# Sampling stage of a four-layer convolution kernel: x distances and column spreads each moved one batch earlier

## The reference, cut to what matters

```
off = conv2d(x, ow, ob).reshape(Bn, K, 2, Hh, Ww)      # K = 9 taps, one y and one x offset each
cy = iy + dy + off[:, :, 0];  cx = ix + dx + off[:, :, 1]
samp = the four neighbours of (cy, cx), weighted bilinearly, zero outside the image
out = einsum('bckhw,ock->bohw', samp, w) + b
h = relu(group_norm1(out)) + x
```

## Time and profile before

| | |
|---|---|
| median of three runs | 881.16 us |
| the profiled execution | 886.09 us |
| its span in the profile | 884.2 us |
| busy in the span | TensorE 658.1 us, VectorE 595.3, ScalarE 464.0, GpSimd 159.3 |
| sampling of layer 0, of layer 1 | about 299 to 505 us, and 571 to 778 us |
| granted TensorE clock, mean | 0.894 of full speed |

### The profile page before, as it was taken

The page is one execution under the profiler, slowest core; times in us unless marked ns, Lnnn a source line. Parts: engine busy times, 40 slices in busy tenths (PEclk is TensorE's granted clock), DMA queues, the critical chain, the costliest instruction groups (busy, mean ns, idle before and its releaser), DMA issues.

```text
span 884.2 us, 30272 instructions
## 1 busy us (share of the span) xinstructions
PE 658.1 (74%) x13944; PEld 453.6 (51%) x13944; DVE 595.3 (67%) x823; ACT 464.0 (52%) x623; POOL 159.3 (18%) x219
## 2 busy tenths in 40 slices
PE   2408999999996848777877769567777777839382
PEld 1103555557873427665555546346555555627151
DVE  6893262121242988888889845697889988886365
ACT  3505344242331666777778541457787788541513
POOL 7000000000023221333330003413332331000000
PEclk9857999999999978999999979969899999969696
DMA  4000000000037864776663006987657664000002
GB/s 159 0 0 1 3 3 2 4 16 4 4 89 232 339 237 173 247 245 215 208 218 122 3 3 175 331 285 241 210 205 232 234 210 160 3 1 4 2 3 96
DMA packets 28778, 108.73 MB, mean 123 GB/s; under 512 B 10612, under 2 KB 15412, under 8 KB 24552
## 3 DMA queue, kind: packets, MB, share of 16 engines
q0 software_dynamic: 14400, 86.80, 28.6%
q1 hardware_dynamic: 14248, 19.97, 7.3%
HBM read 91.84 MB, written 19.65 MB: 126 GB/s over the span
## 4 chain that ended last, share of the span: by engine, by line
PE 49%; DVE 20%; ACT 19%; issue 6%; DMA 4%; SPq 3%; DVEq 0%; ACTq 0%
PE psum L1242 13%; PE psum L1322 10%; PE psum L1345 7%; PE psum L1289 6%; PE psum L1218 5%; ACT arena L1087 4%; ACT arena L1076 4%; PE psum L1434 3%; ACT arena L1088 3%; DMA offsets<-arena 3%; DVE arena L420 3%; DVE arena L737 3%; DVE arena L738 2%; ACT arena L1098 2%; SPq L470 2%
## 5 line engine op out<-in xcount | busy, mean ns | idle before, releaser
L1322 PE MATMUL psum<-arena 64*64 64x297 f32 (+4 forms) x4512 | 245.4, 370 | 101.2 <-DVE arena L420 55.9
L1322 PEld LDWEIGHTS psum<-arena 64*64 64x64 f32 x4512 | 182.9, 146 | 162.2 <-issue 83.7
L1098 ACT ACTIVATE arena<-psum 128x792 f32<-128x792 f32 (+1 forms) x96 | 83.1, 865 | 104.5 <-PE psum L1322 97.3
L1504 POOL DMA_DIRECT2D arena<-offsets_by_batch x128 | 91.1, 723 | 249.6 <-DVE arena L738 187.8
L1242 PE MATMUL psum<-arena 32*32 32x512 f32 x3456 | 115.0, 597 | 0.3 <-DVE arena L660 0.3
L736 DVE SCALAR_TENSOR_TENSOR arena<-arena 128x792 f32<-128x792 f32 (+3 forms) x96 | 92.4, 963 | 14.6 <-ACT arena L1088 14.0
L1289 PE MATMUL psum<-arena 32*32 32x512 f32 x2304 | 83.3, 623 | 18.5 <-issue 12.7
L1242 PEld LDWEIGHTS psum<-arena 32*32 32x32 f32 x3456 | 73.4, 103 | 39.9 <-issue 13.0
L738 DVE SCALAR_TENSOR_TENSOR arena<-arena 128x792 f32<-128x792 f32 (+3 forms) x96 | 92.1, 959 | 0.0
L737 DVE SCALAR_TENSOR_TENSOR arena<-arena 128x792 f32<-128x792 f32 (+3 forms) x96 | 92.1, 959 | 0.0
L1088 ACT ACTIVATE arena<-arena 128x792 f32<-128x792 f32 (+3 forms) x96 | 86.3, 899 | 0.0
(11 more groups left out here) (137 smaller groups left out, 682.9 us busy)
## 6 DMA issues: line engine op xcount, KB each, us to landing
arena<-offsets_by_batch POOLq DMA_DIRECT2D x112, 576.0 KB, 8.1
arena<-offsets_by_batch POOLq DMA_DIRECT2D x16, 624.0 KB, 7.9
offsets<-arena SPq DMA_DIRECT2D x32, 256.0 KB, 8.5
offsets_by_batch<-offsets SPq DMA_DIRECT2D x184, 24.0 KB
arena<-columns POOLq DMA_DIRECT2D x24, 160.0 KB, 9.0
columns<-arena POOLq DMA_DIRECT2D x8, 320.0 KB, 6.8
arena<-in_x SPq DMA_DIRECT2D x4, 512.0 KB, 5.3
out<-arena SPq DMA_DIRECT2D x8, 256.0 KB, 2.2
```

Source lines behind the costliest of these rows:

```text
L1098: ins = a.activation(ap(SAMP + n // 2 % 2 * SPAR + n % 2 * SLOTS * K * SX + u * WB[0], [[SR, 2], [SX, KR], [1, w]]), ap_ps(bank, [[CH, 2], ...
L1322: ins = t_.matmul(ps_t(s, bank + r, first * K * w, many * K * w), window, ap(g_at(unit, d0) + first * TW + s * w, [[GS + TW, many], [SLOTS ...
L1504: g.dma_start(cols(in_at(n, 0), 2 * in_rows(n) * W, 64 * r + 32 * half, 32), bass.AP(batch_d.tensor, 2 * (4 * r * NB + n) * INS, [[0, QW / ...
```

## The change

Three edits are made; nothing is added and nothing is left out.

1. On ScalarE, the distances of batches 0 and 1 are made before the first sample copy. After that the distances of batch n+2 stand behind the y terms that follow the copy of unit (n, 2). Before, they stood one copy later.
2. On VectorE, the spread of batch n+1 stands behind the products of unit (n, 1), for n from 1 to 14. Before, the spread of batch n stood behind the products of unit (n, 0). Its wait for TensorE moves with it: it now waits for the samples of batch n-1 while VectorE is in batch n.
3. On GpSimd's queue, the chunk of columns number n // 2 + 1 is fetched behind the offsets of batch n = 3, 5, 7 and so on. Before, chunk n // 2 was fetched behind those of batch n = 4, 6, 8.

```diff
--- before.py
+++ after.py
@@ -736,8 +736,8 @@
                     v.scalar_tensor_tensor(term(0), term(0), 0.0, part(tx), ALU.min, ALU.mult)
                     v.scalar_tensor_tensor(term(1), term(1), 1.0, part(tx), ALU.subtract, ALU.mult)
                     v.scalar_tensor_tensor(term(2), part(ty), 0.0, part(tx), ALU.min, ALU.mult).then_inc(s_g, 1)
-                    if u == 0 and n >= 2:
-                        spread_windows(L, n)
+                    if u == 1 and 1 <= n < NB - 1:
+                        spread_windows(L, n + 1)
 
             def spread_windows(L, n):
 
@@ -1078,8 +1078,6 @@
             def y_terms(L, unit):
 
                 n, u = divmod(unit, NU)
-                if u == 0:
-                    distances(L, n)
                 if unit >= RING:
                     act.wait_ge(s_un, UNITS * L + unit - RING + 1)
                 part = ap(in_at(n, 1) + u * TW, [[W, in_rows(n)], [1, 2 * WB[u]]])
@@ -1121,10 +1119,12 @@
                     copy_columns(L, g_)
                 copy_offsets(L, 1)
                 copy_offsets(L, 2)
+                distances(L, 0)
                 for unit in range(RING - 1):
                     y_terms(L, unit)
                 copy_offsets(L, 3)
                 y_terms(L, RING - 1)
+                distances(L, 1)
                 act.wait_ge(s_xs[0], 64 * (L + 1))
                 act.wait_ge(s_xs[1], 64 * (L + 1))
                 for unit in range(UNITS):
@@ -1133,9 +1133,11 @@
                             act.wait_ge(s_ds[m], 64 * (L + 1))
                         act.wait_ge(s_red, 4 * (L + 1))
                     copy_samples(L, unit)
+                    n, u = divmod(unit, NU)
                     if unit + RING < UNITS:
                         y_terms(L, unit + RING)
-                    n, u = divmod(unit, NU)
+                    if u == NU - 1 and n + 2 < NB:
+                        distances(L, n + 2)
                     if u == 1 and n % 2 == 0 and n >= 2:
                         copy_rows(L, n // 2 - 1)
                 copy_rows(L, NM - 1)
@@ -1517,8 +1519,8 @@
                 for n in range(NB):
                     if n >= 2:
                         load_batch(L, n)
-                    if n >= 4 and n % 2 == 0:
-                        load_windows(L, n // 2)
+                    if n >= 3 and n % 2 == 1 and n // 2 + 1 < NCHUNK:
+                        load_windows(L, n // 2 + 1)
 
             pool.wait_ge(s_xa, 3 * NCH)
             g.memset(ap(XP3, [[PW, 4 * RP], [PW - 1, 2]]), 0.0)
```

## The result

The changed kernel takes 842.27 us (median of four runs, 836.00 to 846.81); the kernel before takes 881.73 us beside it (four runs, 880.79 to 883.46). The ratio is 0.9545, with a 95% interval of 0.9479 to 0.9612: faster by 4.6%. The forecast was 841.5 us.

The account below looks back on a forecast made before the run. A ring with VectorE's spread before TensorE's even unit bounds the kernel; its period falls from 24.13 to 21.7 us. Starts, six periods and ends save 19.9 + 19.8 = 39.7 us, 881.16 to 841.5; range 837 to 866.

Parts of the forecast that it names:

- The ring: Loop of waits from one even batch's TensorE unit through contraction, ScalarE and VectorE to the next: 21.5 us after the change.
- VectorE's own work: VectorE's busy time in each two-batch period, claimed to stay at 21.60 us and to be nearest its limit.
- period 21.7: Time per two batches in the sampling stages, claimed to fall from 24.13 to 21.7 us, bounds 21.6 and 22.2.
- mutual loss: Allowance in the period for the ring and VectorE's work delaying each other; up to 22.2 us if both lose.
- The idle time of 2.0 us: TensorE's wait before an even batch's unit, claimed to shrink from 3.99 to 2.0 us, giving the full clock.
- The sum of 39.7 us: Total gain claimed over both layers: 19.9 us in layer 0 and 19.8 in layer 1.
- border work: Extra 1.7 us of the first batches within six periods; 0.8 us of it was kept in the forecast.
- the 1.52 us wait: VectorE's wait for ScalarE's odd-batch distances behind TensorE's even unit, claimed to go when the distances move ahead.
- The low clock: Rival at TensorE's even unit: clock stays low, period 23.25 us, gain 17.6, time 863.6; chance 0.22 including a mix.
- The wait only changes its name: Rival: products before the spread are held up as long by ScalarE, so no gain, 881 us; chance 0.05.
- The load: Rival at ScalarE's distances before the copy: landing slows to 24 us, period 25.5, time 900 us; chance 0.05.
- 3 us of cover: Margin between an offset load's landing, 12.9 us at worst, and ScalarE's distances, due 16 to 18 us after issue.

Follow-up runs that it names:

- the extra copy: Changed kernel plus one ScalarE copy of 576 columns per even batch, between the copy of (E, 1) and its y terms: 849.52 us.
- 1 us less for VectorE: Changed kernel with three of the four pieces of each odd batch's spread made by ScalarE instead of VectorE: 848.68 us.
- the spreads on GpSimd: Changed kernel with the spreads of the even batches made by GpSimd instead of VectorE: 860.54 us.
- the kernel with the idle time filled: Kernel before, with 14 unused matmuls of 80 columns on TensorE ahead of each unit that opens an even batch: 865.33 us.
- distances alone: Kernel before with only the first edit, ScalarE's distances one copy earlier; spread and chunks as before: 877.13 us, ratio 0.9915.
- the second trace: The changed kernel, unaltered, profiled and timed again: 846.69 us, ratio 0.9584.
- the three traces of after: The changed kernel, unaltered, profiled three times; timed at 842.27, 846.69 and 841.69 us.
- both edits: Changed kernel with the contraction put behind unit (E, 1) and three pieces of each odd batch's spread made by ScalarE: 854.20 us.
- spreads and chunks alone: Kernel before with the second and third edits, distances left behind the copy: 845.04 us, ratio 0.9574.

## Why the prediction was right

**The ring and VectorE's own work, period 21.7.** Right, and for the reason given: the two lie within 0.1 us of each other. The period is 21.57 us in every pair of batches of this trace but the first (22.0). Only their order is the other one. I took VectorE's 21.60 for the longer, and it is the ring: the extra copy in it costs its full 0.57, and 1 us less for VectorE brings nothing. VectorE's own work is 21.47, read from the spacing of its instructions, so without any ring only 0.10 us a period more could be had. The 0.1 us that I added for mutual loss did not come.

**The idle time of 2.0 us and the clock.** The clock is 1.00, as forecast. The idle time is 1.81, since one term was off: I took 2.1 for TensorE's last unit, and it lasts 2.27, so 1.39 + 2.69 - 2.27 = 1.81. That 0.2 us mattered more than I knew. The rows of before put the edge between 2.07 and 2.83 us; in the experiments the low level came after idle times from 1.95 us on, and the full one still after 2.74. At 2.0 the call was closer than the 0.22 for this rival suggests, and that it held in every period was in part luck.

**The sum of 39.7 us.** The traces have 42.4. Up to (2, 0), counted from the tents of batch 1, 3.05 and 2.7 us went (forecast 2.6 each). In the six periods 16.6 and 16.5 went (15.5 and 15.4): the mis-sized term is the 21.7, 6 x 0.13 = 0.8 a layer, and the rest is border work that shrank too (0.45 us where I kept 0.8). At the end 1.6 and 1.9 went (1.8). The median of the runs fell by 39.5 us; its interval (34 to 46 us) does not tell the two sums apart.

**The waits.** As forecast, VectorE's waits for the distances are gone, and 1.3 and 1.5 us are left for y terms. The spread's new wait for TensorE costs nothing: no such wait is in the trace. But I credited the distances' edit with the 1.52 us wait of each pair, and that was the wrong owner: once the spread is moved, the old order of distances shows one wait of 0.5 us. The sum was right because it came from the ring and not from adding up waits.

**The rivals.** The low clock did not come. It was a real danger: with the spreads on GpSimd it came back in part, and the kernel with the idle time filled puts its worth at 17.4 us, where this rival had 22. "The wait only changes its name" is false for the whole change and true for one of its parts: distances alone bring 5.6 us of 40. The load does not bind, but I judged it too safe. It lands after 12.8 us at most, against the 18.3 that the three buffers allow; what is nearer is the distances' place. I forecast 3 us of cover there, and 0.45 was left, 0.02 in the second trace. I had the landing at 10.1 and left out the 0.6 us from the last product to the first issue.

## What to carry to other kernels

Do not add up an engine's waits: price a reordering by the ring, one trip from an instruction back to itself in the next period, and compare it with the work of the busiest engine. What stands directly in front of the engine that the ring waits for is worth moving first; the longest wait in the list (here the distances, 15 to 18 us a layer) may hang on it and go by itself. And look at what idle time is left before TensorE after the change, since the clock of the next unit can depend on it. Look as well at how much time is left between the landing of a load and its first reader: here the longest load had come within 0.5 us of it, and no list of waits shows that.

## What the runs showed of the hardware

- Idle time of TensorE between its units goes with the granted clock of what follows, but does not decide it alone. Before an even unit, after 1.81 us it was 1.00 in every period of the three traces of after. After 1.95 us (both edits, layer 1) it was 0.61. After 2.12 to 2.19 us it was 1.00 in some periods and 0.56 to 0.72 in others of the same kernel, and after 2.43 us 0.57 in two and 1.00 in two. After 2.34 us (distances alone) it was 0.59, after 2.67 and 2.74 us (spreads and chunks alone) 1.00, and after 3.31 us (distances alone) 0.50. After 3.54 us and more it was 0.50 to 0.65 in every period. The values below 1.00 are means over a unit that starts at the low level (1.2 GHz) and mostly ends at the full one. What else decides it was not found out.
- Filling such idle time with matmuls whose results nobody reads gave 17.4 us of 882 without any other change.
- GpSimd needs 2.1 us for a `tensor_scalar` of 384 fp32 columns of which VectorE makes four in 1.40 us, and beside each such GpSimd instruction one VectorE instruction takes 0.3 us longer (0.98 became 1.28 to 1.31).
- Instructions that follow without a wait overlap at their ends: VectorE's products of 0.98 us start every 0.90, and ScalarE's copy of 0.68 us holds the next one back by 0.57. A wait shorter than the overlap leaves the engine looking busy all through.
- The timed runs of after went from 836.00 to 847.88 us over the three comparisons, while the sampling stages of its three profiled executions differed by 0.4. A stage cut out of the trace was the finer measure here, and what moves the other stages is open.
